# Order of the last retention tile and of the two MoE fronts in a float32 macaron block on one Trainium2 core

## The reference

```
x = x + 0.5 * ffn(layernorm(x))        # MoE
x = x + attn(layernorm(x))             # two retention layers
x = x + 0.5 * ffn(layernorm(x))        # MoE, the same weights

ffn(h):  probs = softmax(h @ router_w + router_bias); top 2 of 16, weights renormalised
         routed = sum over 15 experts of weight * (silu(h @ gate_e) * (h @ up_e)) @ down_e, the 16th gives h back
         shared = silu(causal conv of 3 taps over h) * (h @ shared_up) @ shared_down
attn(x): twice: x += (retention(layernorm(x)) * silu(xo)) @ reto_w + reto_b
                x += gelu(layernorm(x) @ ffn1_w + ffn1_b) @ ffn2_w + ffn2_b
         then layernorm with lnf_g, lnf_b
```

## Time and profile before

| | |
|---|---|
| runs | 1527.48, 1531.32, 1531.19 us; median 1531.19 |
| profiled execution | 1527.78 us |
| its span on the core | 1525.9 us |
| mean granted clock of TensorE | 0.95 |
| busy over the span | PE 1339.6 (88%), PEld 1098.0 (72%), DVE 1028.3 (67%), POOL 648.9 (43%), ACT 596.3 (39%) |

### The profile page before, as it was taken

The page is one execution under the profiler, slowest core; times in us unless marked ns, Lnnn a source line. Parts: engine busy times, 40 slices in busy tenths (PEclk is TensorE's granted clock), DMA queues, the critical chain, the costliest instruction groups (busy, mean ns, idle before and its releaser), DMA issues. The chain is left out here.

```text
span 1525.9 us, 30606 instructions
## 1 busy us (share of the span) xinstructions
PE 1339.6 (88%) x11824; PEld 1098.0 (72%) x11824; DVE 1028.3 (67%) x2359; ACT 596.3 (39%) x1006; POOL 648.9 (43%) x508
## 2 busy tenths in 40 slices
PE   3899998478999999999998999999998637999993
PEld 2479995267888887887887887887787524699962
DVE  5854664768777777867767777877775377556634
ACT  6335664213343334234344233334333345266630
POOL 4765505524232232424334342543461455755045
PEclk9899999779999999999999999999999868999997
DMA  9987757500000000000010000000000051577544
GB/s 335 360 273 253 242 169 228 177 15 1 2 1 2 1 2 2 1 2 32 12 56 2 1 15 2 16 15 2 15 15 1 14 194 45 186 247 235 189 151 138
DMA packets 109323, 139.18 MB, mean 91 GB/s; under 512 B 11776, under 2 KB 95616, under 8 KB 109184
## 3 DMA queue, kind: packets, MB, share of 16 engines
q1 hardware_dynamic: 94784, 101.56, 20.4%
q0 software_dynamic: 12288, 33.57, 6.6%
q10 hardware_dynamic: 2112, 2.10, 0.4%
HBM read 71.66 MB, written 65.54 MB: 90 GB/s over the span
## 5 line engine op out<-in xcount | busy, mean ns | idle before, releaser
L1603 DVE TENSOR_TENSOR l_probs<-l_banks,l_past 128x512 f32<-128x512 f32 x256 | 159.9, 681 | 33.9 <-PE l_banks L1793 33.6
L1462 POOL TENSOR_TENSOR l_g_lo<-l_q,l_g_hi 128x1024 fp32r<-128x1024 f32 x16 | 53.8, 3361 | 266.3 <-ACT l_g_hi L1377 266.3
L79 PE MATMUL l_w_ps<-l_w_hi,l_f_hi 128*128 128x256 f32 x512 | 152.5, 298 | 15.7 <-DVE l_f_lo L1634 13.9
L1386 ACT ACTIVATE l_act_f<-l_w_ps,l_ffn_b 128x512 f32<-128x512 f32 x128 | 88.2, 689 | 190.6 <-PE l_w_ps L81 184.5
L80 PE MATMUL l_w_ps<-l_w_lo,l_f_hi 128*128 128x256 f32 x512 | 145.8, 285 | 0.0
L81 PE MATMUL l_w_ps<-l_w_hi,l_f_lo 128*128 128x256 f32 x512 | 145.7, 285 | 0.0
L79 PE MATMUL l_w_ps<-l_b_hi,l_w_hi 128*128 128x512 f32 x256 | 110.3, 431 | 13.4 <-POOL l_b_lo L1458 13.4
L79 PEld LDWEIGHTS l_w_ps<-l_w_hi,l_f_hi 128*128 128x128 f32 x512 | 99.0, 193 | 25.2 <-DVE l_f_lo L1634 23.0
L1634 DVE TENSOR_TENSOR l_f_lo<-l_act_f,l_f_hi 128x512 fp32r<-128x512 f32 x128 | 98.6, 818 | 18.1 <-ACT l_f_hi L1387 18.1
L597 POOL DMA_INDIRECT a_picked<-rows,a_pos_i x64 | 64.3, 1005 | 90.8 <-issue 69.5
L81 PE MATMUL l_w_ps<-l_b_hi,l_w_lo 128*128 128x512 f32 x256 | 102.0, 398 | 0.0
(11 more groups left out here) (376 smaller groups left out, 4022.1 us busy)
## 6 DMA issues: line engine op xcount, KB each, us to landing
rows<-a_zeros SPq DMA_DIRECT2D x15, 1024.0 KB, 12.6
a_xb<-rows SPq DMA_DIRECT2D x46, 256.0 KB
rows<-a_yb SPq DMA_DIRECT2D x46, 256.0 KB, 3.1
b_xb<-rows SPq DMA_DIRECT2D x46, 256.0 KB, 3.3
rows<-b_yb SPq DMA_DIRECT2D x46, 256.0 KB, 2.6
a_w_in<-in_moe_w SPq DMA_DIRECT2D x15, 384.0 KB, 12.7
b_w_in<-in_moe_w SPq DMA_DIRECT2D x15, 384.0 KB, 8.4
l_w<-in_ffn_w SPq DMA_DIRECT2D x8, 512.0 KB, 6.9
```

Of the source, the lines that this page charges most:

```text
L79: tensor.matmul(out, w_hi, x_hi, start=start, stop=False)
L1386: nc.scalar.activation(act_f[:, f, :], w_ps[:, f % 2, :], ACT.Gelu, bias=ffn1_b[:, b.layer, f:f + 1]).then_inc(act_done, 1)
L1603: dve.tensor_tensor(probs[c % 2][:, r * w:(r + 1) * w].rearrange("p (h n) -> p h n", n=P), banks[:, r, :].rearrange("p (h n) -> p h n", n= ...
```

## The change

**Retention, last tile.** PE makes the first quarter of `feed_out(14)` ahead of `project_out`, two quarters behind it, and the last behind `turn_b`. The low part of the last tile (`low_b(15)`) is made by DVE instead of POOL. ACT roots and DVE normalises tile 13 before DVE adds the retention, so `finish(13)` can start earlier on POOL. One `low_feed` goes behind the last `gate_result` and the others ahead of it. The hidden layer of tile 15 is made in other PSUM banks, so it no longer waits for the feed-forward sum of tile 14. `feed_out(15)` signals each sub-tile, and DVE measures and finishes sub-tile by sub-tile (`measure_last`, `finish_last`), with the root for each on ACT. Old x and lnf_b for tile 15 are joined beforehand: SP loads old x to `last_old` (the memory of `xn2`) once `turn_b` is through, POOL adds lnf_b.

**Fronts, in both MoE stages.** PE: `count(0)` goes ahead of the turnings of tiles 6 and 7; `shared_in(2)` ahead of `count(1)`; `shared_down(1)` to `(3)` behind `shared_in(3)`. DVE: all four low parts ahead of `plan(1)`, `weigh(1)` and `place_blocks(1)` right behind `place(1)`, `add_shared(0)` and the others later. POOL: the low parts of pieces 9 and 10 between the two scatters instead of ahead of both.

```diff
@@ moe, gpsimd
-                for n in range(POOL_LO):
-                    if n < POOL_HI:
-                        high_weights(n)
+                for n in range(POOL_HI):
+                    high_weights(n)
                     low_weights(n)
-                for b in range(HALVES):
-                    scatter(b)
+                scatter(0)
+                for n in range(POOL_HI, POOL_LO):
+                    low_weights(n)
+                scatter(1)
@@ moe, vector
-                low_weights(POOL_LO)
+                for n in range(POOL_LO, PIECES):
+                    low_weights(n)
                 plan(1)
                 place(1)
+                weigh(1)
+                place_blocks(1)
                 add_shared(0)
                 shared_product(2)
-                for n in range(POOL_LO + 1, PIECES):
-                    low_weights(n)
-                weigh(1)
-                place_blocks(1)
-                add_shared(1)
                 shared_product(3)
-                add_shared(2)
-                add_shared(3)
+                for t in range(1, FRONT):
+                    add_shared(t)
@@ moe, tensor
                 route(1)
+                count(0)
                 turn(6)
                 turn(7)
-                count(0)
...
                 shared_in(1)
+                shared_in(2)
                 count(1)
                 shared_down(0)
-                shared_in(2)
-                shared_down(1)
                 shared_in(3)
-                shared_down(2)
-                shared_down(3)
+                for t in range(1, FRONT):
+                    shared_down(t)
@@ retention
+        def hidden_ps(b, f):
+            return banks[:, f % 2, :] if b.n == final.n else w_ps[:, f % 2, :]
+
+        def fed_ps(b, s):
+            return (w_ps[:, s, 0:D] if s < 2 else rm_ps[:, s - 2, 0:D]) if b.n == final.n else feed_ps[:, s, :]
@@ retention, sync
-                with sp.Fori(1, NT) as t:
+                for t in range(1, NT - 1):
                     sp.wait_ge(final_done, t)
                     sp.dma_start(x_old[:, :, :], view[t]).then_inc(x_old_in, 16)
+                sp.wait_ge(bT_done, final.n + 1)
+                sp.dma_start(last_old[:, :, :], view[NT - 1]).then_inc(last_old_in, 16)
@@ retention, scalar (a is None)
-                        root("f", b)
+                        _, mv, std = norms["f"][:3]
+                        for s in range(SUB):
+                            act.wait_ge(last_var, s + 1)
+                            nc.scalar.activation(std[:, s:s + 1], mv[:, s, 1:2], ACT.Sqrt, bias=eps[:, :]).then_inc(last_std, 1)
@@ retention, scalar (more == 0)
+                        root("f", after(b, -1))
                         root("2", a)
-                        root("f", after(b, -1))
@@ retention, gpsimd (a is None)
+                        pool.wait_ge(last_old_in, 16)
+                        carry(3)
+                        pool.tensor_tensor(last_old[:, :, :], last_old[:, :, :], normf[:, 1:2, :].broadcast_to([P, SUB, D]),
+                                           ALU.add).then_inc(last_old_done, 1)
                         finish(after(b, -1))
...
-                    low_b(a)
+                    if more:
+                        low_b(a)
                     add_bias(a, 1, xn2_done, fed)
@@ retention, vector
+                def measure_last(s):
+                    stats, mv = norms["f"][:2]
+                    dve.wait_ge(last_fed, s + 1)
+                    dve.wait_ge(fed, final.n + 1)
+                    link(dve.tensor_tensor(tile_of(final, s), tile_of(final, s), fed_ps(final, s), ALU.add))
...
+                    link(dve.bn_stats(stats[:, s, :], tile_of(final, s)))
...
+                    dve.bn_aggr(mv[:, s, :], stats[:, s, :]).then_inc(last_var, 1)
+
+                def finish_last(s):
+                    _, mv, std, rstd = norms["f"][:4]
+                    dve.wait_ge(last_std, s + 1)
+                    dve.wait_ge(last_old_done, 1)
+                    dve.reciprocal(rstd[:, s:s + 1], std[:, s:s + 1]).then_inc(last_step, 1)
...
+                    link(dve.scalar_tensor_tensor(tile_of(final, s), tile_of(final, s), mv[:, s, 0:1], normf[:, 0, :],
+                                                  ALU.subtract, ALU.mult))
+                    dve.scalar_tensor_tensor(tile_of(final, s), tile_of(final, s), rstd[:, s:s + 1], last_old[:, s, :],
+                                             ALU.mult, ALU.add).then_inc(final_done, 1)
...
                         normalise_f(after(b, -1))
-                        add_feed(b)
-                        measure_final(b)
+                        for s in range(SUB):
+                            measure_last(s)
+                            if s == 1:
+                                finish_last(0)
+                            if s == 2:
+                                finish_last(1)
+                                finish_last(2)
+                        finish_last(SUB - 1)
...
+                        if more == 0 and b is not None and c == SUB - 1:
+                            for f in FEEDS[c - 1] + FEEDS[c][:1]:
+                                low_feed(b, f)
+                            gate_result(a, c)
+                            continue
...
                     if more == 0:
+                        measure_final(after(b, -1))
+                        normalise_f(after(b, -1))
                         add_retention(a)
                         measure_retained(a)
-                        measure_final(after(b, -1))
                         normalise_2(a)
                         scale_b(a)
-                        normalise_f(after(b, -1))
+                        low_b(a)
                         add_feed(b)
                         return
@@ retention, tensor
                     if a is None:
                         for f in range(KF):
                             feed_in(a, b, f)
+                        pe.wait_ge(added, b.n)
                         feed_out(b)
                         return
...
                     if more == 0:
+                        feed_out(b, range(0, 1))
                         project_out(a, last_state)
-                        feed_out(b)
+                        feed_out(b, range(1, 3))
                         turn_b(a)
+                        feed_out(b, range(3, SUB))
                         return
```

More of the change, by code:

```diff
@@ L1635, in low_feed, with low_b @@
                                       ALU.subtract).then_inc(f_lo_done, 1)
+                def low_b(t):
+                    dve.wait_ge(b_hi_done, t.n + 1)
+                    dve.tensor_tensor(b_lo[:, :, :], full[:, :, :], b_hi[:, :, :].bitcast(F32), ALU.subtract).then_inc(b_lo_done, 1)
                 def add_retention(a):
@@ L1727, in _ @@
                 steps(dve, step)
-                last = whole(NL * NT - 1)
-                normalise_f(last)
-                for r, op in ((0, ALU.mult), (1, ALU.add)):
-                    dve.wait_ge(xf_done, NT + r)
-                    dve.tensor_tensor(tile_of(last), tile_of(last),
-                                      normf[:, r:r + 1, :].broadcast_to([P, SUB, D]), op).then_inc(xf_done, 1)
-                dve.wait_ge(xf_done, NT + 2)
-                dve.wait_ge(x_old_in, 16 * NT)
-                dve.tensor_tensor(tile_of(last), tile_of(last), x_old[:, :, :], ALU.add).then_inc(added, 1)
             @block.tensor
@@ L1852, in feed_in, with feed_out @@
                         w = slice(f * P, (f + 1) * P)
-                        last = split3(pe, w_ps[:, f % 2, :], w1_hi[:, k, w], w1_lo[:, k, w], b_hi[:, k, :], b_lo[:, k, :],
+                        last = split3(pe, hidden_ps(b, f), w1_hi[:, k, w], w1_lo[:, k, w], b_hi[:, k, :], b_lo[:, k, :],
                                       k == 0, k == KD - 1)
                     last.then_inc(ffn1_done, 1)
-                def feed_out(b):
+                def feed_out(b, subs=range(SUB)):
                     pe.wait_ge(f_hi_done, KF * (b.n + 1))
@@ L1860, in feed_out @@
                         weights_ready(pe, b.layer, FFN2)
-                    for s in range(SUB):
+                    for s in subs:
                         t = slice(s * P, (s + 1) * P)
```

29 lines of the change are left out of this document (21 added, 8 removed).

## The result

The changed kernel takes 1517.2 us (median of 5 runs, 1516.5 to 1522.1) beside 1531.2 before: a ratio of 0.9923, 95% interval 0.9902 to 0.9944. The medians are 14.0 us apart; the ratios, which go by all runs and not by the two medians alone, make it 11.8 and 13.0 us. So I take it as faster by 12 to 13 us; forecast were 19.7. By the first ratio the changed kernel stands at 1519.4 us, just above the forecast range of 1503.5 to 1518.5. Its profiled execution took 1516.48 us, the span 1514.4.

The account below looks back on a forecast made before the run. TensorE, busy 88% of the span, was taken as the bound. Profiled 1527.8 - 20.8 (last retention tile) + 1.1 (both fronts) = 1508.1, so 1511.5 us against the median; range 1503.5 to 1518.5.

Parts of the forecast that it names:

- The last retention tile: Last tile of retention to DVE's end: 1233.2 - 1212.4 = 20.8 us gained, between 17.5 and 24.
- normalise_2 held by the third operation of finish(13): Last retention tile: DVE's normalise, ready at 1174.8, may be held by POOL until about 1177.1; 1177 taken.
- the free 1210.0: DVE's end after the last sum if no POOL operation holds finish_last: the low bound.
- the held 1212.4: DVE's end with one remaining POOL operation of finish(14), 2.3 us, put in front of finish_last's backlog.
- S in the first front: Start of shared_in(0) in the first stage: 54.3, 5.0 us later than the 49.36 before.
- POOL's low parts behind scatter(0) ... nothing: Both fronts: moved low parts end by 88.5 and 1310.5, before PE's first turn_x needs them, so cost nothing.
- the 1.81 and 3.22 us: Earlier trace's small DVE operations, slowed beside POOL; the move was to take both off DVE's plan and place.
- The look-out: Skill's rule cited for finish_last: GpSimd and two-SBUF-input VectorE instructions lock each other out; 1.81 us against 0.17 agrees.
- T = S + 41.8: Both fronts: shared_in(0)'s start to first turn_x falls from 44.0 to 41.8, 2.2 us less, between 0.5 and 3.5.
- In the second front S: Start of shared_in(0) in the second stage: 0.95 us later, as count(0) moves ahead of two turnings.
- S 5.0 later: First front: turnings queued behind the waiting count(0) start shared_in(0) 5.0 us later, bounds 3.5 and 7.
- the first front loses more: Rival, first front: half clock lasts into shared_in(0), S + 7, DVE late to add_shared(0); +5 us, 1516.5; chance 0.14.

Follow-up runs that it names:

- e9: Changed kernel's last retention tile with all expert fronts of the kernel before, on a faster chip: ratio 0.9871, 1509.1 us.
- e15: Changed kernel with POOL's two late low parts ahead of scatter(0) again in both stages, on a faster chip: ratio 0.9867, 1508.9 us.
- e16: As e15, with count(0) also behind turn(7) again, on a faster chip: ratio 0.9853, 1506.7 us.
- e1: Changed kernel with POOL's two late low parts ahead of scatter(0) in the first stage alone, on a 1708 us chip: ratio 0.9872.
- e4: Same kernel as e9 (new last retention tile, all fronts of before), on a slower chip (1703 to 1708 us): ratio 0.9877.
- e12: Same kernel as e16 (low parts ahead of scatter(0), count(0) behind turn(7)), on a slower chip (1703 to 1705 us): ratio 0.9836.

## Why the prediction was wrong

**Right.** The last retention tile, point by point: project_out at full clock behind the quarter; normalise_2 held by the third operation of finish(13); the hidden layer at 1181.8 in the old frame (forecast 1182), the eighth GELU at 1193.95 (1193.5), the last sum at 1206.7 (1206.3), the end at 1211.0, between the free 1210.0 and the held 1212.4. The gain is 22.2 us in the trace from the last retain matmul to DVE's end, 20 us in the time of e9; forecast 20.8. S in the first front at 54.40 (54.3), scatter(0) at 53.23 (52.8), no wait before count(1).

**Wrong: "POOL's low parts behind scatter(0) ... nothing".** I looked only at who waits for the low parts, not at what runs beside them. By the prediction's own numbers they end by 88.5, so begin at about 85, and DVE is through place_blocks(1) and add_shared(0) at S + 32.6 = 86.9, so in the midst of them at 85; and the 1.81 and 3.22 us of the earlier trace rows, which I took off as relief in the old place, are the same hold that waited in the new one. Its price against e15 is 3.4 us of waiting (3.52 and 0.16) and, by the three downs (9.2 us together and 7.3), 1.9 of low clock: 5.3 us in the front, some 7 by the ratios. In the sum this term was nothing. With the hold out, e15's 0.9867 is 1510.8 us beside 1531.2: within a microsecond of the forecast. The earlier trace rows had even the length, beside POOL's row in the second front of the kernel before:

```profile
1273.65 3.72 POOL L579 TENSOR_TENSOR b_w_lo<-b_w_in,b_w_hi 128x768 fp32r<-128x768 f32 x2 [9.86 <-ACT b_w_hi L464]
```

The two low parts ended at 1277.37, and the 3.22 us that began at 1274.36 at 1277.58, past both.

**The look-out was too narrow.** The prediction speaks of VectorE instructions with two SBUF inputs and says that the 1.81 us agree. That row is a TENSOR_SCALAR with one tensor input, and so is the one held for 3.56 us. What agrees with a lock by whole instructions is the length, 1.81 us, that of one low part; whoever looks for two-input operations alone passes over both rows.

**Wrong in size: "T = S + 41.8".** Each last down behind an add was right, 2.08 and 1.41 us of waiting between them; that these waits bring the low clock to a down of the three was not in it. It measured 43.3 to 44.5 without a hold, so the 2.2 us gained a front were -0.5 to 0.7. In the second front S came 1.8 us later where the sum has 0.95.

**Right in size, wrong in worth: S 5.0 later.** The sum charged it in full, less 0.5. On the faster chips e15 and e16 show 0.3 us of it at the next stage. The two last errors have opposite signs and about cancel; that e15 comes within a microsecond of the forecast is in part luck.

The rival "the first front loses more" gave 1516.5, close to the result, but by another mechanism (S + 7, DVE late): S was on time.

## What to carry to other kernels

When work of GpSimd is moved to a free slot, lay VectorE's queue beside that slot and ask what stands behind each small SBUF operation that falls into it: its price is up to the length of GpSimd's work, however small it is itself. How the two meet can differ between two stages with the same code (0.07 and 1.34 us behind), and for a like meeting there were two outcomes (0.65 and 2.31 us), so one profile need not show them all. And a gain ahead of a fixed event (here the end of scatter(1)) has to be followed up to that event before it is counted.

## What was not expected

- A VectorE operation of 54 or 20 elements was held for the whole of two GpSimd instructions in a row (3.56 and 3.62 us for 3.56 us of low parts). In other fronts VectorE was let in between the two: 0.65 us in the changed kernel's second, and in the first front of the kernel before, where the 1.81 us of the earlier trace rows ended with the first low part and the next operation was held by the second (1.75). The Trainium skill, SBUF — State Buffer, section "Who interferes with whom", has the lock by whole instructions; that it need not be given up between two is what these rows add.
- On the chips of 1703 to 1708 us the fronts stood still for long with nothing in the trace to wait for. ACT of e1, for one:

```profile
76.14 0.60 ACT L474 ACTIVATE a_sg<-a_gu_ps 128x512 f32<-128x512 f32 x1 [6.60 <-issue]
115.61 0.60 ACT L474 ACTIVATE a_sg<-a_t_ps 128x512 f32<-128x512 f32 x1 [38.88 <-remote]
```

Its input was ready at 86.5 us. S to T was 97 to 104 us in 8 of the 11 fronts there that had the low parts ahead of scatter(0) and 52 to 58 in all 9 that had them behind it; the three short ones of the 11 (e4's first, e12's both, 53 to 68 us) had count(0) behind the turnings. So on such a chip the late low parts may be what pays; the changed kernel itself didn't run there, and the cause wasn't found.
